# A four-layer graph network on one core: casts and a scaling moved to POOL, zero products ahead on PE

## The reference

```python
def _L0_gnn_ref(x, adj, W, a_src, a_dst):          # layer 1 is the same with its own weights
    h = jnp.einsum('bnf,of->bno', x, W)
    e = (h @ a_src)[:, :, None] + (h @ a_dst)[:, None, :]
    e = jax.nn.leaky_relu(e, negative_slope=0.2)
    e = jnp.where(adj == 0, jnp.float32(-1e9), e)
    return jnp.einsum('bij,bjo->bio', jax.nn.softmax(e, axis=-1), h)

def _L2_gnn_ref(hidden, adj, a0, ..., bias):       # with adj of zeros and ones only a0 counts
    e0 = leaky(jnp.einsum('bid,bjd->bij', hidden * a0[:, 0], hidden))
    alpha = sigmoid(where(adj == 1, e0, -max))
    return jnp.einsum('bij,bjd->bid', alpha, hidden) + bias

def _L3_gnn_ref(x, adj, relation, weight, bias):   # relation is adj; only weight[0] counts
    return einsum('bnd,do->bno', einsum('bnm,bmd->bnd', adj == 1, x), weight[0]) + bias

x = _layernorm(x + _L0_gnn_ref(...)); x = _layernorm(x + _L1_gnn_ref(...))
x = _layernorm(x + _L2_gnn_ref(...)); x = _layernorm(x + _L3_gnn_ref(...))
```

## Time and profile before

| | |
|---|---|
| median of 3 runs | 272.94 us (271.94 to 273.21) |
| the profiled execution | 267.62 us, of which the span from first to last instruction is 265.8 us |
| DVE busy | 246.7 us (93%), 956 instructions |
| PE busy | 232.5 us (87%) |
| ACT busy | 217.7 us (82%) |
| POOL busy | 139.3 us (52%), 161 instructions |
| HBM | 17.17 MB read, 4.19 MB written |

### The profile page before, as it was taken

The page is one execution under the profiler, slowest core; times in us unless marked ns, Lnnn a source line. Parts: engine busy times, 40 slices in busy tenths (PEclk is TensorE's granted clock), DMA queues, the critical chain, the costliest instruction groups (busy, mean ns, idle before and its releaser), DMA issues.

```text
span 265.8 us, 6017 instructions
## 1 busy us (share of the span) xinstructions
PE 232.5 (87%) x1799; PEld 205.9 (77%) x1799; DVE 246.7 (93%) x956; ACT 217.7 (82%) x626; POOL 139.3 (52%) x161
## 2 busy tenths in 40 slices
PE   3878969899998999999999999999999969996850
PEld 3767758689877888889897889898999769786740
DVE  1799999999999989999999999999999999999883
ACT  1637526788999999899999999999999979987841
POOL 1001105312485483788766617554697556778851
PEclk9999999999999999999999999999999999999985
DMA  6787470000070005524000542103000110000033
GB/s 237 280 253 240 138 273 27 1 2 0 9 271 1 2 0 128 192 60 179 0 2 2 197 155 86 42 1 122 0 0 2 39 44 27 13 2 1 4 118 123
DMA packets 12147, 21.79 MB, mean 82 GB/s; under 512 B 1104, under 2 KB 5968, under 8 KB 12112
## 3 DMA queue, kind: packets, MB, share of 16 engines
q1 hardware_dynamic: 11680, 21.17, 23.8%
q10 hardware_dynamic: 432, 0.20, 0.3%
HBM read 17.17 MB, written 4.19 MB: 80 GB/s over the span
## 4 chain that ended last, share of the span: by engine, by line
DVE 50%; PE 26%; issue 9%; ACT 5%; POOL 5%; DMA 3%; DVEq 0%; POOLq 0%; ACTq 0%
PE banks L1123 11%; DVE wgt_all L808 11%; DVE fstats L856 9%; DVE fres L849 7%; DVE fres L841 5%; POOL frstd L542 4%; PE banks L1064 4%; DVE wgt_all L815 3%; PE banks L1089 3%; DVE raw_all L731 2%; PE banks L1120 2%; DMA adj_all<-adj_turned 2%; DVE top L783 2%; PE banks L1081 1%; PE banks L1100 1%
## 5 line engine op out<-in xcount | busy, mean ns | idle before, releaser
L542 POOL TENSOR_TENSOR frstd<-fvar,minus_half 128x4 f32<-128x4 f32 x64 | 73.7, 1157 | 102.0 <-DVE fvar L862 35.1
L1123 PE MATMUL banks<-vals_all,wgt_all 128*128 128x129 f32 x512 | 63.3, 277 | 3.5 <-DVE wgt_all L808 3.5
L1123 PEld LDWEIGHTS banks<-vals_all,wgt_all 128*128 128x128 f32 x512 | 59.6, 191 | 5.3 <-issue 3.1
L808 DVE SCALAR_TENSOR_TENSOR wgt_all<-banks,gain,maskT 128x256 f32<-128x256 f32 x128 | 52.5, 472 | 1.0 <-PE banks L1081 0.9
L538 POOL TENSOR_TENSOR xb<-xs_all,bias_cen 128x256 f32<-128x256 f32 x60 | 44.9, 772 | 8.6 <-DVE xs_all L765 4.4
L856 DVE BATCH_NORM_STATS2 fstats<-fres 128x6 f32<-128x256 f32 x128 | 47.6, 413 | 0.0
L1089 PE MATMUL banks<-fxT,fxTa 128*128 128x256 f32 x128 | 35.8, 382 | 0.0
L1123 PE MATMUL banks<-xs_all,wgt_all 128*128 128x128 f32 x256 | 31.6, 277 | 4.8 <-DVE wgt_all L815 4.7
L1123 PEld LDWEIGHTS banks<-xs_all,wgt_all 128*128 128x128 f32 x256 | 29.9, 192 | 5.4 <-issue 3.2
L640 ACT ACTIVATE xs_all<-fres,frstd 128x128 f32<-128x128 f32 x96 | 30.9, 427 | 2.0 <-POOL frstd L542 1.8
L637 ACT ACTIVATE xs_all<-fres,fcenter,frstd 128x128 f32<-128x128 f32 x64 | 26.5, 497 | 3.8 <-DVE fcenter L873 3.7
(11 more groups left out here) (93 smaller groups left out, 440.0 us busy)
## 6 DMA issues: line engine op xcount, KB each, us to landing
adj_all<-adj_turned SPq DMA_DIRECT2D x16, 512.0 KB, 4.8
xT_all<-x_turned SPq DMA_DIRECT2D x16, 256.0 KB, 4.4
x_all<-x_laid SPq DMA_DIRECT2D x16, 256.0 KB, 4.0
out<-xs_all SPq DMA_DIRECT2D x16, 256.0 KB, 2.3
bias<-biases_laid SPq DMA_DIRECT2D x1, 128.0 KB, 3.3
w_pack<-W_and_columns ACTq DMA_DIRECT2D x1, 68.0 KB, 2.7
w_fast<-W_turned ACTq DMA_DIRECT2D x1, 64.0 KB, 3.7
w_nat<-in_L_gnn_W ACTq DMA_DIRECT2D x1, 64.0 KB, 5.5
```

The lines of the kernel that those rows point to most:

```text
L542: nc.gpsimd.tensor_tensor(frstd[:, int(l), slot(n), :], fvar[:, int(l), slot(n), :], minus_half[:, :, :], ALU.pow).then_inc(fast_pool[k], 1)
L808: last = nc.vector.scalar_tensor_tensor(out=wgt(u)[:, c, :], in0=place(f"rows{l}", u), scalar=gain[:, u, c, 1:2], in1=maskT(u)[:, c, :], o ...
L1123: last = nc.tensor.matmul(place(f"out{l}", u)[:, b * width:(b + 1) * width], wgt(u)[:, c, b * P:(b + 1) * P], (vals if l in "01" else xs)( ...
```

## The change

Four things. `raw` moves from DVE to POOL in 15 of 16 teams (all but team 10). `mask` moves from ACT to POOL in 14 of 16 teams (all but teams 1 and 3), as `x * 1 + 0`. `xTa` moves from ACT to POOL in all teams: it no longer reads PSUM but the copy `fxT` that `xT2` has made, so the bank is free after `xT2`, and `score` waits for POOL. PE first multiplies zeros: 9 products of 128x128 ahead of `projection_weights(0)` and 4 behind it. `ORDER` and `BANKS` are written anew for all engines. In the new order `norm2` is on DVE for 2 teams (5 before), `norm3` on DVE for 4 (3 before), and `bias2` on DVE for 2 (0 before); `low` and `bias3` stay at 1 and 2. The switches between the exponential and the sigmoid table on ACT are 20 (18 before).

```diff
@@ load_adj (SP)
-                    sp.wait_ge(fast_dve[(n - ADJ) % K], at("dve", "raw", final(n - ADJ)))
+                    rawer = doer("raw", n - ADJ)
+                    sp.wait_ge(signals[rawer][(n - ADJ) % K], at(rawer, "raw", final(n - ADJ)))
@@ POOL
+            def make_raw(l, n, k):
+                pool.wait_ge(fast_adj_in[n % ADJ], loaded(n * H, ADJ))
+                for u in graphs(n):
+                    if n >= RAW:
+                        pool.wait_ge(fast_pe[(n - RAW) % K], at("pe", "score", u - RAW * H))
+                        pool.wait_ge(seen_step, SEEN.index(n - RAW) + 2)
+                    nc.gpsimd.tensor_scalar(raw(u), adj_in(u), -1.0, 1.0, ALU.mult, ALU.add).then_inc(fast_pool[k], 1)
+
+            def make_mask(l, n, k):
+                pool.wait_ge(fast_adj_in[n % ADJ], loaded(n * H, ADJ))
+                if n >= MASK:
+                    pool.wait_ge(fast_pe[(n - MASK) % K], at("pe", "agg", final(n - MASK)))
+                for u in graphs(n):
+                    nc.gpsimd.tensor_scalar(maskT(u)[:, :, :], adj_in(u), 1.0, 0.0, ALU.mult, ALU.add).then_inc(fast_pool[k], 1)
+
+            def scaled_xT(l, n, k):
...
+                for u in graphs(n):
+                    pool.wait_ge(fast_act[k], at("act", "xT2", u))
+                    nc.gpsimd.tensor_scalar(fxTa(u)[:, :], fxT(u)[:, :], a2[:, 0:1], None, ALU.mult).then_inc(fast_pool[k], 1)
@@ ACT
-            def copy_xTa(l, n, k):
...
-                    nc.scalar.activation(fxTa(u)[:, :], place("xT2", u), ACT.Copy, scale=a2[:, 0:1]).then_inc(fast_act[k], 1)
@@ PE
-                        "xT2": (fast_act, "act", "xTa"), "score": (fast_act, "act", "sigmoid"),
+                        "xT2": (fast_act, "act", "xT2"), "score": (fast_act, "act", "sigmoid"),
@@ scores (PE)
-                    pe.wait_ge(fast_act[k], at("act", "xTa", u))
+                    pe.wait_ge(fast_pool[k], at("pool", "xTa", u))
+                    rawer = doer("raw", n)
+                    pe.wait_ge(signals[rawer][k], at(rawer, "raw", u))
@@ PE, the start of the sequence
+            def idle_products(count):
+                for _ in range(count):
+                    nc.tensor.matmul(banks[:, 5, 0:P], zero[:, :], zero[:, :], start=True, stop=True)
+
+            pe.wait_ge(zero_set, 1)
+            idle_products(9)
             projection_weights(0)
+            idle_products(4)
```

More of the change, by code:

```diff
@@ L461, in loaded @@
             return u // (depth * H) * 16 + 16
+        SEEN = [n for name, l, n in order("dve") if name == "seen"]
         signals = {"pe": fast_pe, "act": fast_act, "dve": fast_dve, "pool": fast_pool}
@@ L547, in low_part @@
                     nc.gpsimd.tensor_tensor(lo(u)[:, :, :], xs(u)[:, :, :], hi(u)[:, :, :], ALU.subtract).then_inc(fast_pool[k], 1)
-            steps = {"bias": biases, "pow": powers, "low": low_part}
+            def make_raw(l, n, k):
[12 more added lines that the diff above has]
+            def scaled_xT(l, n, k):
+                if n == first("pool", "xTa"):
+                    pool.wait_ge(w0_in, 16)
+                if n >= FXTA:
+                    pool.wait_ge(fast_pe[(n - FXTA) % K], at("pe", "agg", final(n - FXTA)))
+                for u in graphs(n):
+                    pool.wait_ge(fast_act[k], at("act", "xT2", u))
+                    nc.gpsimd.tensor_scalar(fxTa(u)[:, :], fxT(u)[:, :], a2[:, 0:1], None, ALU.mult).then_inc(fast_pool[k], 1)
+            steps = {"xTa": scaled_xT, "raw": make_raw, "mask": make_mask, "bias": biases, "pow": powers, "low": low_part}
             for step, l, n in order("pool"):
@@ L597, in values @@
                     last.then_inc(fast_act[k], 1)
-            def copy_xTa(l, n, k):
-                if n == first("act", "xTa"):
-                    act.wait_ge(w0_in, 16)
-                if n >= FXTA:
-                    act.wait_ge(fast_pe[(n - FXTA) % K], at("pe", "agg", final(n - FXTA)))
-                for u in graphs(n):
-                    nc.scalar.activation(fxTa(u)[:, :], place("xT2", u), ACT.Copy, scale=a2[:, 0:1]).then_inc(fast_act[k], 1)
             def sigmoids(l, n, k):
@@ L641, in normalize @@
                     last.then_inc(fast_act[k], 1)
-            steps = {"mask": make_mask, "xT": copy_xT, "gains": gains, "vals": values, "xTa": copy_xTa, "sigmoid": sigmoids,
+            steps = {"mask": make_mask, "xT": copy_xT, "gains": gains, "vals": values, "sigmoid": sigmoids,
                      "high": high_part, "agg": copy_gathered, "norm": normalize}
@@ L731, in make_raw @@
                     nc.vector.tensor_scalar(raw(u), adj_in(u)[:, :, :], -1.0, 1.0, ALU.mult, ALU.add).then_inc(fast_dve[k], 1)
-            SEEN = [n for name, l, n in order("dve") if name == "seen"]
             def note_seen(l, n, k):
-                dve.wait_ge(fast_dve[k], at("dve", "raw", final(n)))
+                rawer = doer("raw", n)
+                dve.wait_ge(signals[rawer][k], at(rawer, "raw", final(n)))
                 dve.wait_ge(seen_step, SEEN.index(n) + 1)
```

## The result

The changed kernel takes 274.74 us (median of 4 runs, 274.38 to 275.18), beside 272.44 (270.07 to 273.21) for the kernel before in runs of the same batch: ratio 1.017, interval 1.0119 to 1.0222. The two medians alone give 1.008, for three of these four executions of before took 271.9 us or more; in the four later batches its median was 269.4 to 271.2 us, and a version of the changed kernel with one load moved (the last experiment) has 1.0167 beside 27 executions of it. The ratios leave out executions that lie over 1.5% above the fastest of their kernel. Forecast were 268.4 us and a gain. The profiled execution took 274.57 us with a span of 272.7; those of before are 267.62 and 265.8, so the spans differ by 6.9 us, more than the medians do.

The account below looks back on a forecast made before the run. DVE was taken to bound the kernel, with PE nearly as full. Terms of -13.5 (DVE's work), +8.5 (stops) and +0.5 (start) gave -4.5 us, from 272.94 to 268.4 us; range 261.5 to 276.0.

Parts of the forecast that it names:

- DVE bounds the kernel: Whole kernel: DVE, busy 246.7 of 265.8 us, is the fullest engine, a little ahead of PE at 232.5.
- I take +8.5: DVE instructions blocked while POOL reads large tiles: stops put at 9 us now, to grow by 8.5 us.
- DVE's own terms: Work moved on or off DVE: raw -12.8 us, norms -2.4, bias2 +1.7, in sum -13.5 us.
- the forecast's own range: Spread of the main forecast, 263.4 to 271.5 us (chance 0.50), from stops of +5 to +14 and start of -0.8 to +1.5.
- never free for DVE: Shared port pair of DVE and POOL: a POOL cast in place of an ACT cast always costs DVE something.
- So DVE's work is worth its full price: 60 to 240 us: work taken off DVE shortens the time fully until PE's 7.8 us of idle time are used up.
- the second rival: PE is really full, DVE's freed time turns into idle time, and nothing is gained: 271.6 to 274.3 us, chance 0.16.
- ACT's relief counted at nothing: ACT falls from 217.7 to about 192 us busy, stays off the path, and is credited with no gain.
- POOL near 203 us: POOL's busy time rises from 139.3 to about 203 us, with casts at 0.88 us and xTa at 0.49.
- The start: Zero products before the first projection: between -0.8 us and +1 or a little more, taken as +0.5 us.
- POOL is late with `pow`: Casts queued ahead of pow delay DVE and PE by 9 us in sum, giving 277 us; chance 0.22.
- The prediction's sign for it: POOL's cast above 1.2 us, or over 5 us of new waits for pow by center, logits1 or ACT's norm, means slower.

Follow-up runs that it names:

- The extra scalings of a constant tile: Kernel before, xTa still on ACT, with two added POOL scalings of a constant 128x256 tile per team that nothing reads: ratio 1.0108 (1.001 to 1.0206).

## Why the prediction was wrong, step by step

**DVE bounds the kernel: right.** Less work on DVE alone gives 2% (0.9795), and `raw` given back to it in the changed kernel costs 2.8%.

**"I take +8.5" for the two engines in each other's way: the step that failed, by its size.** Against the -13.5 us of DVE's own terms, its busy time rose by 1.6: the term is 15.1 us, 6.6 more than taken. Of these, 1.4 us are the price of the moved steps and no stops: neighbours on DVE overlap at their ends, so that the 32 `raw` casts are 12.4 us of busy time and not 32 x 426 ns = 13.6. By busy time DVE's own terms are -12.1 us (11.6 and 2.0 less, 1.5 more), and the stops 13.7 us, still 5.2 more than taken. Half of the 15.1, 7.6 us, comes from `xTa` and `mask` (both on ACT, 240.7); the other 7.5 are in the raw casts on POOL and the new order, where norms cost 409 for 303 ns (24 of them, 2.5 us) and the additions of a bias 628 for 417 (8 of them, 1.7 us). In the old order `raw` on POOL freed 6.2 us of its own 13.6 (32 x 426 ns). I had scaled the stops by POOL's time of large tiles and priced the moved DVE steps at their old means; yet those steps, and the ones that used to be clear, now meet POOL more often, for POOL idles less before `pow` (102.0 to 37.0 us). An estimate from the two traces bears this out. Each DVE instruction's time above the least of its group is put down to the POOL instruction that it overlaps longest: the moved casts and `xTa` then hold DVE for 10.9 us in the changed kernel, and POOL's additions and subtractions, hardly changed in number, for 19.2 where they held it for 13.8. The upper bound of the forecast's own range, 14 us, is about what was measured. Nor did the sum follow its own factors: twice 9 us, less a seventh, less the present 9 is +6.4, not +8 to +9. And "never free for DVE" was too wide, as the norms at 246.64 us show.

**"So DVE's work is worth its full price": wrong in part.** Predicted was idle time up by 0.5 us, at the start; it rose by 5.3. That and the 6.6 make the 11.4 us between -4.5 and +6.9. `raw` alone on POOL freed 6.2 us of busy time and at most 1% of time, since 14 of its instructions lie in the first 60 us, where DVE then waits for PE's chain (idle 8.3 to 11.1 us). That is the second rival's mechanism, in the first 60 us rather than in the middle. Where the rest of the idle time comes from is open. PE's two stretches at the lower clock are in it, with an unknown share, and undoing both moves off ACT still leaves 1.0068.

**ACT's relief counted at nothing: right, and its price was missed.** What left ACT brought nothing and cost stops on DVE: 1.0117 for `mask`, 1.0332 for `xTa` in the old order, about 1.0% for both in the new one. (ACT's own sum was 6 us short: 198.2 us, not 192.)

**POOL near 203 us: right (200.8) for wrong reasons.** A cast is 0.65 to 0.70 us, not 0.88; `xTa` is 0.97, not 0.49.

**The start: right within a microsecond, and no gain.** +0.5 us was taken; the first `weight0` came 0.33 us earlier, and over the kernels with zeros it lies between 0.8 us earlier and 1.0 later, so the sign in this execution is luck. Ahead of the first `pow` stand fourteen casts (seven steps of two), not the ten that the prediction and the text ahead of it count; at the 0.65 to 0.70 us measured they are some 9 us, near the 8.8 taken.

**The rival "POOL is late with `pow`": its side was right, its mechanism only a small part.** The prediction's sign for it, more than 5 us of new waits for `pow`, was met by ACT's norms, and yet it is not what costs most. DVE's waits for `pow` fell (`center` 1.2 to 0.3 us); ACT's norms wait 5.8 us longer in sum. With `mask` alone put back they still wait the same 7.6 us, with `xTa` alone put back 3.1, and the ratios of these two (1.0125 and 1.0118) don't differ.

## What to carry to other kernels

Before moving work to POOL beside a full DVE, price the stops from DVE's mean durations less their least ones, and count each moved POOL microsecond against DVE, also when it comes from a third engine: here 68.7 us of casts and scalings on POOL, with the new order, cost DVE 14 to 15 us, more than the 12 to 13.5 that it had been relieved of. Work taken from an engine that is not the bound buys nothing to set against that. Price a step by its busy time in the trace and not by its mean duration, where neighbours overlap. And before two small gains are compared or added, look at the granted clock of every execution: here it went with some 4 us for the same kernel, more than either small gain of the old order.

## What the runs showed of the hardware that was not expected

- On POOL a `tensor_scalar` with immediate numbers over 512 columns, int32 to bf16, takes 0.65 to 0.70 us on average; the one whose factor is a column of the tile (`w_pack`), over 256 columns of f32, takes 0.97. Per column that is nearly three times as much; the two differ in type and in the kind of factor, and no run tells these apart. The extra scalings of a constant tile show the same price, so it isn't contention with the copy:

```profile
L565 POOL TENSOR_SCALAR extra<-w_pair,w_pack 128x256 f32<-128x256 f32 x32 | 31.4, 990 | 0.0
```

- POOL instructions that only write hold DVE's `tensor_scalar` as well, and a run of four held one to the run's end (1.98 us for 0.43).
- PE's first passes run at the lower of its two clock levels whatever they multiply: 18 passes of zeros take 4.05 us, 0.225 each, twice the 112 ns of the earlier trace rows, and behind them the first projection has 0.13 a pass, where without them it had 0.26.
- Late in the kernel a wait of PE can cost its clock: behind 2.98 us of waiting for DVE, 16 products ran at the lower level and took 3.10 us instead of 2.02. Behind 2.82 us in an execution of the kernel before, the level stayed.
